# Logits and attention weights kept tap-innermost in SBUF, in a two-layer convolution kernel on one core

## The chip, the cores and the metric

One core of one Trainium2 chip runs the whole batch. The time is device microseconds from the first to the last instruction of one execution; lower is better.

## What is computed

The input x is (32, 56, 56, 96) in float32. Two residual layers follow each other:

```
x = x + L0(group_norm(x))      # outlook attention, 12 heads of 8 channels, 3x3 taps, stride 2
x = x + L1(group_norm(x))      # depthwise 3x3 with the signs of the weights

L0: v = x @ W_v;  the 3x3 patch of v around each of 28x28 windows
    a = mean of each 2x2 pixels of x @ W_a + b_a   -> per window and head a 9x9 matrix
    a = softmax(a * scale) over its last axis (9 taps)
    out[q] = sum_k a[q, k] * v[k];  the 9 outputs are added back to the image at their places
    y = folded @ W_o + b_o
```

What matters here is the matrix a: per image 784 windows, and for each 12 heads x 9 rows q (108 partitions) with 9 taps k.

## The kernel before

One program per engine, each a loop over the images; a body of the loop has 64 slots (g), one per pair of terms of the attention sum. An image goes through a pipeline of stages in three neighbouring bodies: input and logits (`s1`), attention (`s2`), the depthwise layer and output (`cv`). The image is cut into two halves h: half 0 has 15 rows of windows (420 windows), half 1 has 14 (392).

In each slot TensorE broadcasts two weight planes from `stack` to 96 channels (`broadcast`, L733), VectorE multiplies them with the values (`product`, L600, into one of four buffers `prod`), GpSimd adds the two products of 45 of the 64 slots (`pre_add`, L363), and three slots later TensorE multiplies with W_o and accumulates (`add_up`, L753). VectorE waits for the broadcast and for a free buffer; TensorE waits for the pre-added product.

Everything else is put between the slots by hand: the table `AT` names for every kind of piece the slots after which it is issued (numbers from 64 on lie in the next body). Each engine executes in order, and every piece counts up a semaphore that later pieces on other engines wait for. The softmax of one half of one image is this chain:

- logits: TensorE, one matmul per tap (L698) into one of two PSUM banks `side`; ScalarE drains each with the bias into `att[h]` (L433), 9 per half, at slots 19 to 23 for half 0 and 39 to 53 for half 1
- maximum: VectorE, 4 reductions per half over the 9 taps (L623), each a quarter of the windows; slots 24 to 27 and 56 to 58
- less the maximum: GpSimd, 9 pieces (L345); exponential: ScalarE, 3 pieces (L464)
- sum: VectorE, 4 reductions (L627), slots 36 to 39 and 70 to 73; inverse: VectorE, 2 reciprocals (L631); scaled by ScalarE (L467)
- times the inverse: GpSimd, 9 pieces (L351), slots 44 to 49 and 75 to 84
- split into two float16 parts: the first part by ScalarE (L475, 3 pieces), the second part = att - first part by GpSimd (L356, 9 pieces), slots 48 to 54 and 81 to 88
- SyncE copies both parts into `stack` (L283, L289, 12 transfers per half), from which the next attention stage broadcasts.

`att[h]` is laid out as 9 tap planes of 420 or 392 windows, so a piece of GpSimd or ScalarE is one plane or three. A reduction over the taps therefore steps from plane to plane: 1680 bytes in half 0, 1568 in half 1.

On VectorE there are also 24 taps of the depthwise layer per image (L647, both inputs in SBUF), and the additions of a finished class into X1 (L611). ScalarE loads the next image from PSUM (L440), drains the values (L426), starts X1 and ACC and runs the norms; GpSimd adds pixels for the pooling (L332, L338) before the multiplications of half 1.

## Time and profile before

| | |
|---|---|
| median of 3 runs | 5119.74 us (5117.42 to 5121.8) |
| span of the profiled execution, its own time | 5120.9 us |
| TensorE busy | 4119.3 us (80%) |
| VectorE busy | 4730.3 us (92%) |
| ScalarE busy | 2005.6 us (39%) |
| GpSimd busy | 4037.2 us (79%) |
| mean granted TensorE clock | 0.850 of full |

PE is TensorE (PEld its weight loads), DVE VectorE, ACT ScalarE, POOL GpSimd, SP SyncE. Busy time is the union of an engine's instruction times; an instruction that is held up after it has started counts as busy. One image takes about 156 us, so 32 images and some filling make the span.

### The profile page before, as it was taken

The numbers are of one execution on the slowest core, as the hardware profiler recorded it, in microseconds if no ns is written. First come the engines' busy times: TensorE is split into PE (matmuls) and PEld (weight loads), VectorE is DVE, ScalarE is ACT, GpSimd is POOL, SyncE is SP. The second block draws the span as 40 slices with busy tenths as digits, with TensorE's granted clock in tenths as the row PEclk, the third lists the DMA queues.
The fourth block names the chain that finished last, engine by engine and source line by source line (L and its number), as shares of the span: only waits on it lengthen the run. The fifth ranks groups of instructions, "written<-read, shape, count | busy, mean of one in ns | idle before, by whom it ended". The sixth has DMA issues, their size and how long they took to land.

```text
span 5120.9 us, 55367 instructions
## 1 busy us (share of the span) xinstructions
PE 4119.3 (80%) x13632; PEld 2114.1 (41%) x13632; DVE 4730.3 (92%) x3723; ACT 2005.6 (39%) x2753; POOL 4037.2 (79%) x3628
## 2 busy tenths in 40 slices
PE   4877887878887888878788887888878888878885
PEld 2434444434444344444344443444434444434442
DVE  5799999999999999999999999999999999999997
ACT  4424444334443344432444433444324444334431
POOL 5787877877877888778878788787787787887883
PEclk7988888888888788888888888888888888888887
DMA  1110111101111111111011111111110111111111
GB/s 39 38 38 24 47 44 37 47 21 40 47 33 47 36 25 47 42 39 47 21 40 47 33 47 30 31 47 38 43 47 15 46 47 33 47 24 37 47 29 28
DMA packets 126083, 194.36 MB, mean 38 GB/s; under 512 B 14248, under 2 KB 115464, under 8 KB 122472
## 3 DMA queue, kind: packets, MB, share of 16 engines
q1 hardware_dynamic: 97384, 155.50, 13.0%
q10 hardware_dynamic: 28672, 38.55, 2.5%
q8 instruction: 11, 0.18, 0.0%
q14 instruction: 16, 0.13, 0.0%
HBM read 39.22 MB, written 38.54 MB: 15 GB/s over the span
## 4 chain that ended last, share of the span: by engine, by line
POOL 45%; issue 25%; PE 18%; ACT 5%; DVE 5%; DMA 1%; SPq 0%; DVEq 0%; POOLq 0%; ACTq 0%; PEldq 0%; PEld 0%
POOL prod L363 15%; POOL part L356 10%; POOL att L351 10%; PE acc L753 10%; POOL att L345 6%; PE bc L733 4%; DVE prod L600 2%; ACT X L440 2%; POOL pc L332 2%; PE side L698 2%; ACT X L523 2%; PE side L692 1%; DVE ACC L647 1%; PE side L710 1%; DVE top L631 1%
## 5 line engine op out<-in xcount | busy, mean ns | idle before, releaser
L753 PE MATMUL acc<-prod,wo 96*96 96x392 f32 x5312 | 2478.5, 573 | 161.8 <-POOL prod L363 155.7
L600 DVE TENSOR_TENSOR prod<-bc,VAL 96x784 f32<-96x784 f32 x2048 | 1928.2, 959 | 307.5 <-PE bc L733 289.4
L363 POOL TENSOR_TENSOR prod<-prod 96x392 f32<-96x392 f32 x1440 | 1685.5, 1178 | 501.3 <-DVE prod L600 491.7
L733 PE MATMUL bc<-stack,sel 96*96 96x392 f16 x4608 | 1303.2, 378 | 633.5 <-DVE prod L600 611.5
L647 DVE SCALAR_TENSOR_TENSOR ACC<-XP,sg,ACC 96x1064 f32<-96x1064 f32 (+1 forms) x768 | 1736.2, 2281 | 14.9 <-ACT ACC L534 13.8
L753 PEld LDWEIGHTS acc<-prod,wo 96*96 96x96 f32 x5312 | 982.1, 188 | 675.1 <-issue 271.6
L733 PEld LDWEIGHTS bc<-stack,sel 96*96 96x96 f16 x4608 | 576.2, 137 | 1571.4 <-DVE prod L600 972.2
L351 POOL TENSOR_TENSOR att<-att,top 108x420 f32<-108x420 f32 (+1 forms) x576 | 750.3, 1321 | 38.3 <-ACT top L467 38.3
L345 POOL TENSOR_TENSOR att<-att,top 108x420 f32<-108x420 f32 (+1 forms) x576 | 645.1, 1138 | 144.2 <-DVE top L623 144.2
L356 POOL TENSOR_TENSOR part<-att,part 108x420 f16<-108x420 f32 (+1 forms) x576 | 737.3, 1298 | 0.0
L433 ACT ACTIVATE att<-side,ba 108x420 f32<-108x420 f32 (+1 forms) x576 | 340.5, 597 | 671.6 <-PE side L698 659.0
L698 PE MATMUL side<-pooled,wa 96*108 96x392 f32 (+1 forms) x1152 | 528.0, 573 | 46.3 <-ACT att L433 23.2
L627 DVE TENSOR_REDUCE top<-att 108x105 f32<-108x945 f32 (+1 forms) x256 | 456.9, 1796 | 14.5 <-ACT att L464 14.5
L623 DVE TENSOR_REDUCE top<-att 108x105 f32<-108x945 f32 (+1 forms) x256 | 449.3, 1786 | 15.4 <-ACTq L247 13.2
L426 ACT ACTIVATE VAL<-side 96x392 f32<-96x392 f32 (+1 forms) x256 | 124.7, 512 | 857.5 <-DVE prod L600 713.5
L475 ACT ACTIVATE part<-att 108x1260 f16<-108x1260 f32 (+1 forms) x192 | 234.5, 1221 | 470.4 <-POOL att L351 470.2
L698 PEld LDWEIGHTS side<-pooled,wa 96*108 96x108 f32 x1152 | 221.6, 197 | 305.4 <-issue 224.0
L446 ACT ACTIVATE tok_out<-side 112x384 f32<-112x384 f32 x224 | 110.2, 492 | 605.7 <-PE side L710 304.6
L464 ACT ACTIVATE att<-att 108x1260 f32<-108x1260 f32 (+1 forms) x192 | 232.4, 1210 | 140.5 <-POOL att L345 140.5
L692 PE MATMUL side<-XN,wv 96*96 96x392 f32 (+1 forms) x512 | 244.1, 573 | 7.8 <-ACT tok_out L446 3.8
L370 POOL TENSOR_TENSOR gve<-eps,gvar 96x1 f32<-96x1 f32 x64 | 13.2, 206 | 281.8 <-ACT spill L451 268.8
L440 ACT ACTIVATE X<-side 96x448 f32<-96x448 f32 x224 | 204.2, 1000 | 29.4 <-PE side L704 28.2
(55 smaller groups left out, 2183.7 us busy)
## 6 DMA issues: line engine op xcount, KB each, us to landing
stack<-part SPq DMA_DIRECT2D x192, 275.3 KB
stack<-part SPq DMA_DIRECT2D x192, 256.9 KB
tok_in<-in_x SPq DMA_DIRECT2D x32, 1176.0 KB, 9.7
out<-tok_out ACTq DMA_DIRECT2D x224, 168.0 KB, 4.2
stack<-part SPq DMA_DIRECT2D x192, 30.5 KB
stack<-part SPq DMA_DIRECT2D x192, 28.5 KB
X<-in_L_conv_W_a SPq DMA_DIRECT2D x1, 364.5 KB
ACC<-select SPq DMA_DIRECT2D x1, 144.0 KB
```

The source lines that it names most:

```text
L345: nc.gpsimd.tensor_tensor(att[h][:, k, :], att[h][:, k, :], top[h][:, :], ALU.subtract).then_inc(fine_step, 1)
L351: nc.gpsimd.tensor_tensor(att[h][:, k, :], att[h][:, k, :], top[h][:, :], ALU.mult).then_inc(fine_step, 1)
L356: nc.gpsimd.tensor_tensor(low, a4(h)[:, k], high, ALU.subtract).then_inc(fine_step, 1)
L363: nc.gpsimd.tensor_tensor(p[:, 0, :], p[:, 0, :], p[:, 1, :], ALU.add).then_inc(pre_added, 1)
L433: ins = nc.scalar.activation(att[h][:, k, :], bank[0:QN, 0:cols], ACT.Identity, bias=ba[:, k:k + 1])
L600: nc.vector.tensor_tensor(prod[:, g % PRODUCTS, :, :].rearrange("c a (i j) -> c a i j", j=WIN), b, v, ALU.mult).then_inc(prod_ready, 1)
L623: ins = nc.vector.tensor_reduce(top[h][:, c], by_window[:, c, :], AX.X, ALU.max)
L627: ins = nc.vector.tensor_reduce(top[h][:, c], by_window[:, c, :], AX.X, ALU.add)
L647: nc.vector.scalar_tensor_tensor(a, XP[:, r0 + ty:r1 + ty, tx:tx + SIDE], sg[:, t:t + 1], a, ALU.mult, ALU.add).then_inc(tapped, 1)
L698: last = nc.tensor.matmul(bank[0:QN, 0:ROWS[h] * WIN], wa[:, k, :, :], pooled[:, 0:ROWS[h], :], start=True, stop=True)
L733: last = nc.tensor.matmul(bc[g % 2][0:CH, a, 0:UNIT], sel[:, which, :], stack[h][:, qi, ki * TAPS + kj, si:si + HALF, sj:sj + WIN], start= ...
L753: last = nc.tensor.matmul(acc[c % 2][0:CH, 0:UNIT], wo[:, :], prod[:, g % PRODUCTS, a, :], start=first, stop=s == LAST[c] and (g in PRE or ...
```

## The change

`att[h]` is laid out with the windows outside and the 9 taps inside, so the taps of a window are neighbours (4 bytes apart) and the windows 36 bytes apart. The pieces on GpSimd and ScalarE that were planes become groups of window rows (`ROW_CUTS`: two rows or one, so 504 or 252 elements; three of them together make 1260 or 1008). The maximum and the inverse are repeated over the taps by an access pattern with step 0. The logits of a tap are written with a step of 36 bytes, and both float16 parts, whose own layout stays (tap planes), are made from `att` read with that step. The drain of the first logits waits for the last second part of the image before, where each drain waited for that of its own tap. The slots in `AT` are as they were.

```diff
+ROW_CUTS = ((0, 2, 4, 5, 7, 9, 10, 12, 14, 15), (0, 2, 3, 5, 6, 8, 9, 11, 12, 14))
...
-        att = [sb(f"att{h}", [QN, KK, ROWS[h] * WIN]) for h in range(2)]
+        att = [sb(f"att{h}", [QN, ROWS[h] * WIN, KK]) for h in range(2)]
...
         def a4(h):
-            return att[h][:, :, :].rearrange("r k (i j) -> r k i j", j=WIN)
+            return att[h][:, :, :].rearrange("r (i j) k -> r k i j", j=WIN)
+
+        def rows_of(h, n, many=1):
+            return slice(ROW_CUTS[h][n * many], ROW_CUTS[h][(n + 1) * many])
+
+        def columns_of(h, n, many=1):
+            r = rows_of(h, n, many)
+            return slice(r.start * WIN, r.stop * WIN)
+
+        def over_taps(t):
+            return bass.AP(t.tensor, t.offset, [*t.ap, [0, KK]])
...
-                    nc.gpsimd.tensor_tensor(att[h][:, k, :], att[h][:, k, :], top[h][:, :],
+                    c = columns_of(h, k)
+                    nc.gpsimd.tensor_tensor(att[h][:, c, :], att[h][:, c, :], over_taps(top[h][:, c]),
                                             ALU.subtract).then_inc(fine_step, 1)
...
-                    nc.gpsimd.tensor_tensor(att[h][:, k, :], att[h][:, k, :], top[h][:, :],
+                    c = columns_of(h, k)
+                    nc.gpsimd.tensor_tensor(att[h][:, c, :], att[h][:, c, :], over_taps(top[h][:, c]),
                                             ALU.mult).then_inc(fine_step, 1)
...
-                    low, high = (parts[p][:, k, 0:ROWS[h], 0:WIN] for p in (1, 0))
-                    nc.gpsimd.tensor_tensor(low, a4(h)[:, k], high,
+                    r = rows_of(h, k)
+                    low, high = (parts[p][:, :, r, 0:WIN] for p in (1, 0))
+                    nc.gpsimd.tensor_tensor(low, a4(h)[:, :, r], high,
                                             ALU.subtract).then_inc(fine_step, 1)
...
-                    until(act, fine_step, done(FINE, i - 1, LOW, h, k))
-                    ins = nc.scalar.activation(att[h][:, k, :], bank[0:QN, 0:cols],
+                    if k == 0:
+                        until(act, fine_step, done(FINE, i - 1, LOW, h, KK - 1))
+                    ins = nc.scalar.activation(att[h][:, :, k], bank[0:QN, 0:cols],
                                                ACT.Identity, bias=ba[:, k:k + 1])
...
-                    a = att[h][:, 3 * n:3 * n + 3, :]
+                    a = att[h][:, columns_of(h, n, 3), :]
...
-                    ins = nc.scalar.activation(parts[0][:, 3 * n:3 * n + 3, 0:ROWS[h], 0:WIN], a4(h)[:, 3 * n:3 * n + 3],
+                    r = rows_of(h, n, 3)
+                    ins = nc.scalar.activation(parts[0][:, :, r, 0:WIN], a4(h)[:, :, r],
                                                ACT.Identity)
...
-                by_window = att[h][:, :, :].rearrange("r k n -> r n k")
...
-                    ins = nc.vector.tensor_reduce(top[h][:, c], by_window[:, c, :], AX.X, ALU.max)
+                    ins = nc.vector.tensor_reduce(top[h][:, c], att[h][:, c, :], AX.X, ALU.max)
...
-                    ins = nc.vector.tensor_reduce(top[h][:, c], by_window[:, c, :], AX.X, ALU.add)
+                    ins = nc.vector.tensor_reduce(top[h][:, c], att[h][:, c, :], AX.X, ALU.add)
```

## Rows read from the trace of the kernel before

**Rows 1.** The page: busy time and share of the span, by engine.
```profile
PE 4119.3 (80%) x13632; PEld 2114.1 (41%) x13632; DVE 4730.3 (92%) x3723; ACT 2005.6 (39%) x2753; POOL 4037.2 (79%) x3628
```

**Rows 2.** The page: the chain that ended last, share of the span by engine.
```profile
POOL 45%; issue 25%; PE 18%; ACT 5%; DVE 5%; DMA 1%; SPq 0%; DVEq 0%; POOLq 0%; ACTq 0%; PEldq 0%; PEld 0%
```

**Rows 3.** The taps by their line: count, then min/median/max in ns.
```profile
L647 DVE SCALAR_TENSOR_TENSOR ACC<-XP,sg,ACC x768: 1247/2004/6940, 257.4 to 5107.4; 96x1064 f32<-96x1064 f32 x128, 96x1008 f32<-96x1008 f32 x64
```

**Rows 4.** The timeline of VectorE, three taps in a row: start us, us.
```profile
2537.52 10.85 DVE L647 SCALAR_TENSOR_TENSOR ACC<-XP,sg,ACC 96x1064 f32<-96x1064 f32 x3
```

**Rows 5.** One image in stretches A to H: us, busy us by engine.
```profile
core 0: us, PE busy (x) PEld busy (x) DVE busy (x) ACT busy (x) POOL busy (x), PEclk, DMA share, GB/s
2408.90:2417.40 8.50, 7.00 (x36) 4.78 (x36) 8.50 (x8) 2.10 (x5) 5.52 (x6) 0.91 0.57 151
2417.40:2436.20 18.80, 18.80 (x69) 10.54 (x68) 12.24 (x15) 10.23 (x12) 16.77 (x17) 0.86 0.43 109
2436.20:2450.00 13.80, 11.79 (x55) 7.01 (x54) 13.80 (x13) 13.20 (x22) 5.58 (x10) 0.88 0.00 0
2450.00:2482.70 32.70, 28.43 (x89) 13.96 (x89) 30.98 (x23) 19.39 (x27) 29.11 (x27) 0.90 0.04 8
2482.70:2494.00 11.30, 7.98 (x23) 3.50 (x21) 11.30 (x10) 0.00 (x0) 7.94 (x8) 0.85 0.50 111
2494.00:2515.30 21.30, 15.22 (x46) 6.99 (x46) 20.99 (x18) 7.15 (x8) 21.21 (x15) 0.92 0.05 11
2515.30:2533.00 17.70, 14.87 (x49) 7.54 (x49) 17.70 (x17) 3.51 (x6) 10.51 (x11) 0.90 0.00 0
2533.00:2565.20 32.20, 23.18 (x70) 11.14 (x69) 32.10 (x23) 6.98 (x9) 30.12 (x24) 0.79 0.14 34
```

**Rows 6.** VectorE's groups by form: count, then busy us and mean ns of one.
```profile
L600 DVE TENSOR_TENSOR prod<-bc,VAL 96x784 f32<-96x784 f32 x2048 | 1928.2, 959 | 307.5 <-PE bc L733 289.4 <-issue 10.7 <-ACT VAL L426 0.3
...
L623 DVE TENSOR_REDUCE top<-att 108x105 f32<-108x945 f32 x128 | 229.3, 1832 | 2.2 <-ACT att L433 2.1
...
L623 DVE TENSOR_REDUCE top<-att 108x98 f32<-108x882 f32 x128 | 220.0, 1741 | 13.2 <-ACTq L247 13.2
L611 DVE TENSOR_TENSOR X<-acc,X 96x392 f32<-96x392 f32 x256 | 141.1, 551 | 11.2 <-PE acc L753 11.0
```

**Rows 7.** GpSimd's lines, one by one: min/median/max in ns.
```profile
L356 POOL TENSOR_TENSOR part<-att,part x576: 889/951/2069, 79.1 to 4995.3; 108x420 f16<-108x420 f32 x96, 108x392 f16<-108x392 f32 x96
...
L332 POOL TENSOR_TENSOR pc<-X x64: 1483/1584/2462, 24.8 to 4868.6; 96x840 f32<-96x840 f32 x32, 96x784 f32<-96x784 f32 x32
...
L338 POOL TENSOR_TENSOR pooled<-pc x64: 1011/1044/1090, 26.5 to 4871.2; 96x420 f32<-96x420 f32 x32, 96x392 f32<-96x392 f32 x32
...
L363 POOL TENSOR_TENSOR prod<-prod x1440: 998/1016/2104, 101.3 to 5061.3; 96x392 f32<-96x392 f32 x180
```

**Rows 8.** ScalarE's groups by form: a strided and a packed drain.
```profile
L440 ACT ACTIVATE X<-side 96x448 f32<-96x448 f32 x224 | 204.2, 1000 | 29.4 <-PE side L704 28.2 <-ACT X L523 0.2
...
L426 ACT ACTIVATE VAL<-side 96x448 f32<-96x448 f32 x96 | 48.9, 543 | 718.3 <-DVE prod L600 713.5 <-PE side L692 2.8 <-ACT tok_out L446 2.0
```

**Rows 9.** The second parts (L356) in E and H: busy us, count.
```profile
2482.70:2494.00 11.30, 3.52 (x4) 0.85 0.50 111
2533.00:2565.20 32.20, 12.00 (x8) 0.79 0.14 34
```

**Rows 10.** Timelines of ScalarE and VectorE, logits and first maxima of half 0.
```profile
2468.91 1.32 ACT L433 ACTIVATE att<-side,ba 108x420 f32<-108x420 f32 x2 [2.44 <-PE side L698]
2470.12 1.18 ACT L475 ACTIVATE part<-att 108x1176 f16<-108x1176 f32 x1
...
2478.84 1.29 ACT L433 ACTIVATE att<-side,ba 108x420 f32<-108x420 f32 x2
...
2482.74 3.60 DVE L623 TENSOR_REDUCE top<-att 108x105 f32<-108x945 f32 x2
```

**Rows 11.** Timelines of SyncE and VectorE: last copy, first product of half 1.
```profile
2493.03 0.78 SPq L289 DMA_DIRECT2D stack<-part  x1
...
2504.34 0.96 DVE L600 TENSOR_TENSOR prod<-bc,VAL 96x784 f32<-96x784 f32 x1
```

## The prediction, made before the changed kernel was run

> **What bounds the kernel now.** I read the busy shares first. VectorE is busy 92% of the span, TensorE 80%, GpSimd 79% [rows 1]: three engines are near their limit, so the share alone names no bound. The chain of waits says more: 45% of it runs through GpSimd and only 5% through VectorE [rows 2]. The reason shows where both meet. A tap (L647) takes 1.25 us at best and 2.0 in the middle [rows 3], yet three of them in a row lasted 10.85 us [rows 4], with GpSimd busy all the while. A tap reads two operands in SBUF, and so does a GpSimd piece; here they run one after the other. Much of VectorE's 92% is therefore a wait for GpSimd, and where taps stand, the time is the sum of both.
>
> The period of one image is some 156 us. I cut one into eight stretches [rows 5]: A maxima of half 1, B values, C sums and inverses of half 1, D multiplications and second parts of half 1 with taps and the logits of half 0, E maxima of half 0, F subtractions with taps, G sums and inverses of half 0, H multiplications and second parts of half 0 with taps. VectorE is full in A, C, E and G, where the sixteen reductions lie (four in each). TensorE is full in B. GpSimd is nearly full in F and H, and busy 29.1 of 32.7 us in D.
>
> My sum is made per image and times 32, against the profiled span of 5120.9 us; the median of the runs, 5119.74, stands 1.2 below it, which I leave out.
>
> **The reductions (gain).** Before, the nine taps of a window lie 1680 or 1568 bytes apart; after, they are neighbours. A maximum takes 1832 ns for 945 elements and 1741 for 882, 1787 in the mean, and a sum as much within 12 ns [rows 6]. VectorE's operations with short steps take 551 ns for 392 elements and 959 for 784 [rows 6]: 1.04 ns an element and 143 ns beside. By that, 945 elements take 1127 and 882 take 1061, mean 1094. I take 0.69 us saved of each, 2.8 in each stretch. The other bound is nothing saved, if the time belongs to the reduction and not to its step.
>
> What of it reaches the end is what the next engine leaves. A: TensorE is busy 7.0 of 8.5 us, so 1.5. C: ScalarE is busy 13.2 of 13.8 us (loading the next image, starting X1), and GpSimd's pooling and the multiplications queued behind it wait for that, so 0.6. E: TensorE 8.0 and GpSimd 7.9 of 11.3, so 2.8. G: TensorE 14.9 of 17.7, so 2.8. Together 7.7 us an image.
>
> **The second part on GpSimd (loss).** L356 now reads the logits 36 bytes apart, 18 times an image, each 951 ns in the middle [rows 7]. No row shows GpSimd at such a step. L332 reads 8 bytes apart and shows no penalty (784 elements in 1483 ns, against 998 for 392 in L363 [rows 7]). Bounds: nothing, or even -0.26 us (L332's 1.9 ns an element against 2.55, times 406); above, ScalarE's ratio. Its strided write (L440, 112 bytes) takes 1000 ns where a packed one takes 543 [rows 8]: 1.84 times, so 0.80 us more. I take the surcharge per element of VectorE's reductions, the nearest strided read: (1832-1127)/945 = 0.75 ns, times 406 elements = x = 0.31 us. Of the 18 pieces, 4 start in E and 8 in H [rows 9], one in A and so 5 in D. In D and H GpSimd has no cover, 13x = 4.0. In E the 7.9 us of GpSimd grow by 4x past the 8.5 left after the gain: 4x-0.56 = 0.7. In A it is hidden (5.5 us of 8.5). Sum 4.7 us. SyncE's copies into the stack (L283, L289) follow the last piece; the last is issued at 2493.0 us and TensorE's next half feeds a product at 2504.3 [rows 11], so a shift of 1 to 3 us is covered; without that cover it would cost those 1 to 3 us.
>
> **Subtraction and multiplication.** The same elements in nine pieces of 504 or 252 instead of 420 or 392; one operand is repeated nine times. I take nothing. Lower bound: two operands on the same few bytes, as in L332, -0.25 us each, -9 an image. Upper: short runs. L338 reads 14 runs and takes 1011 ns at least, L363 one run and takes 998 [rows 7], about 1 ns a run, so 0.05 us each and 1.8 an image. They lie on the path, without cover.
>
> **ScalarE (small loss).** L433 now writes 36 bytes apart and L475 reads so. By L440 against the packed drain, (1000-543)/448 = 1.02 ns an element [rows 8]: a logits drain goes from 0.6 to 1.04 us, a first part from 1.19 to 2.4. In D, from 2468.9 to 2480.1 us [rows 10], nine drains and two first parts take 7.9 us; they would take 14.2, 3.0 beyond the 11.2 there. The maxima start 2.6 us after the last drain [rows 10], so they come 0.4 late; TensorE, which has two banks for these tiles, waits some 0.6 for drains, and behind it in order stand broadcasts that VectorE needs. I take 1.0 us an image; bounds 0 and 3.0. In H, ScalarE is busy 7 of 32 us and covers it.
>
> **Edits at nothing.** The drain of logits 0 now waits for the last second part of the image before, not for its own. That part is over at the start of A for half 0 and at 2487.6 us for half 1, while those logits come in D and in G: 30 us of cover. Exponentials and first parts wait for three row pieces as they did for three tap pieces. The pieces of 1260 and 1008 elements in the place of 1176 sum to the same.
>
> **Sum.** -7.7 + 4.7 + 1.0 = -2.0 us an image, times 32 = -64: 5057 us. By this formula the change is neither gain nor loss at x = 0.43 (17x - 0.56 = 6.7).
>
> **Rivals.**
> 1. *The second part pays in proportion.* Place: L356 in D, E, H, on GpSimd, with taps behind it. If a strided read costs GpSimd the ratio that it costs VectorE, 1787/1094 = 1.63, x is 0.60: 17x-0.56 = 9.6, net +2.9 an image, +93: 5214. It decides from x = 0.43 on. With ScalarE's 0.80 it is +202: 5323. For it: GpSimd's chain share; against: L332 pays nothing at 8 bytes. Chance 0.17. Between the surcharge and the ratio, a second part half as long again (x = 0.48) gives 17x-0.56 = 7.6, +0.9 an image, +29: 5150, slower too; chance 0.13.
> The Trainium skill, GPSIMD Engine Reference, Performance pitfalls, states that a step over 8 bytes makes a read loop about 50% dearer. By that x is that of the half-as-long-again case, and the change loses; no row here shows such a step.
> 2. *The reductions do not get faster,* their time belonging to the operation. Then 13x + 1.0 = 5.0 an image, +160: 5281. For it: the 63 elements between the two forms cost 91 ns, 1.4 each and not 1.8, so something beside the step is in it; against: 0.7 us more than other operations of the size. Chance 0.10.
> 3. *Reads at 36 bytes are free* on GpSimd and ScalarE. Then -7.7 + 0.5 = -7.2 an image, -230: 4891. For it: L332. Chance 0.16.
> 4. *The gain is all taken elsewhere* (TensorE in A and G, the taps): within 0.2%. Chance 0.04.
>
> **How the numbers follow.** The forecast has 0.40, with 4990 to 5110 as its own range (x from 0.1 to 0.43, ScalarE from 0 to 2). 0.2% is about what a measurement can tell from no change. Faster: 0.38 of the forecast's 0.40 and 0.16, so 0.54. Slower: 0.29 of rival 1's 0.30 (both cases) and 0.10, so 0.39. Same: the rest, 0.07. The range goes from 4870, just below rival 3, to 5290, just above rival 2; it leaves out ScalarE's ratio on GpSimd and a cheap repeated operand, some 2 in 10 with what I have not seen.
>
> **What would show it.** Right: L623 and L627 near 1.1 us, L356 near 1.26, L345 and L351 with the busy time they had, L433 near 1.0, L475 near 2.4; VectorE's share falls under 88%, its wait for TensorE's broadcasts grows, GpSimd's wait for products shrinks, GpSimd's share of the chain rises. Wrong: L356 at 1.4 or more (rival 1), reductions at 1.8 (rival 2), L356 unchanged (rival 3), or L345 and L351 moved by more than 0.1 us in the mean, which would outweigh all the rest.

## The result, and the profile after

The changed kernel takes 5239.57 us (median of 4 runs, 5221.27 to 5259.17) against 5120.71 for the kernel before on the same chip: 1.023 times as long, with a 95% interval from 1.021 to 1.026. It is slower by 119 us, where I had forecast 64 us faster. The profiled execution took 5259.17 us, with a span of 5257.4, which is 136.5 more than the span before.

The page: busy time by engine, and the chain's shares [rows 1, 2].

```profile
span 5257.4 us, 54863 instructions
PE 4145.8 (79%) x13632; PEld 2138.0 (41%) x13632; DVE 4544.1 (86%) x3723; ACT 2400.8 (46%) x2753; POOL 3950.3 (75%) x3628
...
POOL 30%; PE 28%; issue 19%; DVE 8%; ACT 6%; DMA 5%; ACTq 1%; SPq 1%; DVEq 0%; POOLq 0%; PEld 0%; PEldq 0%
```

VectorE is busy 186 us less than before and GpSimd 87 us less. Only ScalarE has more work, and it is the idlest of the four. So the two engines that I had called the limit got lighter, and the kernel got slower.

The groups by form: count, then busy us and mean ns of one, then the idle time before them.

```profile
L662 DVE SCALAR_TENSOR_TENSOR ACC<-XP,sg,ACC 96x1064 f32<-96x1064 f32 x512 | 1401.4, 2738 | 14.8 <-ACT ACC L550 14.0 <-DVE ACC L662 0.8
...
L370 POOL TENSOR_TENSOR part<-att,part 108x504 f16<-108x504 f32 x352 | 575.1, 1638 | 0.5 <-ACT part L491 0.5
L364 POOL TENSOR_TENSOR att<-att,top 108x504 f32<-108x504 f32 x352 | 449.0, 1283 | 36.5 <-ACT top L482 36.5
L357 POOL TENSOR_TENSOR att<-att,top 108x504 f32<-108x504 f32 x352 | 448.9, 1283 | 59.5 <-DVE top L638 59.4
L491 ACT ACTIVATE part<-att 108x1260 f16<-108x1260 f32 x160 | 396.9, 2481 | 312.5 <-POOL att L364 312.5
L448 ACT ACTIVATE att<-side,ba 108x420 f32<-108x420 f32 x288 | 267.7, 1005 | 125.0 <-PE side L713 125.0
L370 POOL TENSOR_TENSOR part<-att,part 108x252 f16<-108x252 f32 x224 | 251.6, 1123 | 0.0
L638 DVE TENSOR_REDUCE top<-att 108x105 f32<-108x945 f32 x128 | 138.6, 1122 | 7.3 <-ACT att L448 7.1
L638 DVE TENSOR_REDUCE top<-att 108x98 f32<-108x882 f32 x128 | 132.5, 1056 | 15.8 <-ACTq L258 15.8
```

L638 answers to L623 before, L448 to L433, L491 to L475, L370 to L356, L357 and L364 to L345 and L351, L662 (the taps) to L647. The reductions take 1122 and 1056 ns, where I had 1127 and 1061. Among the groups that were not touched, the taps of this form grew most: 1222 us before, 1401 after (the other form, 96x1008, fell from 529 to 494).

The waits: us in total, times, the longest.

```profile
POOL prod L377 <- DVE prod L616: 828.2, 523, 7.5
...
DVE prod L616 <- PE bc L748: 550.3, 560, 4.8
```

Before, GpSimd waited 491.7 us for products and VectorE 289.4 us for broadcasts. Both now wait more: no engine is busy throughout, they wait for one another.

**Where in an image.** Each image makes 64 products, one per slot, and their starts show how long every slot took. This table is worked out from them, as a mean over 28 images. The last column is the duration of the five last taps, at slots 50, 50, 52, 53 and 53. The kernels marked * are experiments of the next section.

```
us per image  period  0-13  14-23 24-35 36-47 48-54 55-63 | last five taps
before        156.95  26.40 29.71 32.60 21.90 26.81 19.53 | 2.44 1.95 1.31 2.10 1.95
after         161.88  26.45 29.34 28.13 21.70 33.93 22.34 | 5.07 2.37 1.31 6.92 1.78
*e1           151.05  25.83 30.29 29.98 20.35 26.82 17.78 | 2.44 1.95 1.31 2.10 1.95
*e11          166.04  26.14 30.84 30.93 20.89 35.25 21.98 | 5.68 2.16 1.31 6.68 2.16
*e2           150.23  26.25 28.73 28.16 21.63 27.94 17.52 | 4.04 1.65 1.31 2.08 2.63
*e14          157.27  27.16 33.39 29.58 20.69 29.45 17.00 | 5.48 2.07 1.31 1.31 2.07
*e10          147.89  26.07 28.19 28.23 30.84 15.95 18.61 | taps at 43 to 47, all 1.22 to 1.81
```

Up to slot 47 the changed kernel gains 5.0 us an image. From slot 48 on it loses 9.9. The 4.9 us between them, over 28 images, make up the 137 us that the spans differ by. Two taps carry most of the 9.9: the first at slot 50 went from 2.44 to 5.07 us, and the first at slot 53 from 2.10 to 6.92, for 1.3 us of work each.

The timeline of the changed kernel there shows how. VectorE first, then GpSimd over the same time (start us, us, and in brackets the idle time before it and what ended it).

```profile
2601.91 7.37 DVE L662 SCALAR_TENSOR_TENSOR ACC<-XP,sg,ACC 96x1064 f32<-96x1064 f32 x2
2609.21 1.84 DVE L616 TENSOR_TENSOR prod<-bc,VAL 96x784 f32<-96x784 f32 x2
2610.98 1.31 DVE L662 SCALAR_TENSOR_TENSOR ACC<-XP,sg,ACC 96x1064 f32<-96x1064 f32 x1
2612.21 0.96 DVE L616 TENSOR_TENSOR prod<-bc,VAL 96x784 f32<-96x784 f32 x1
2613.09 8.62 DVE L662 SCALAR_TENSOR_TENSOR ACC<-XP,sg,ACC 96x1064 f32<-96x1064 f32 x2
```
```profile
2602.16 0.61 POOL L364 TENSOR_TENSOR att<-att,top 108x252 f32<-108x252 f32 x1
2602.74 1.40 POOL L370 TENSOR_TENSOR part<-att,part 108x504 f16<-108x504 f32 x1
2604.10 1.02 POOL L377 TENSOR_TENSOR prod<-prod 96x392 f32<-96x392 f32 x1
2605.07 3.15 POOL L370 TENSOR_TENSOR part<-att,part 108x252 f16<-108x252 f32 x2
2611.13 2.03 POOL L377 TENSOR_TENSOR prod<-prod 96x392 f32<-96x392 f32 x1 [2.91 <-DVE prod L616]
2613.12 2.12 POOL L370 TENSOR_TENSOR part<-att,part 108x504 f16<-108x504 f32 x2
2615.21 1.01 POOL L377 TENSOR_TENSOR prod<-prod 96x392 f32<-96x392 f32 x1
2616.18 4.47 POOL L370 TENSOR_TENSOR part<-att,part 108x504 f16<-108x504 f32 x3
2623.56 1.02 POOL L377 TENSOR_TENSOR prod<-prod 96x392 f32<-96x392 f32 x1 [2.91 <-DVE prod L616]
```

The pair of taps from 2601.91 lasts until GpSimd has nothing left that is ready. The first tap takes 5.07 us of it: four pieces begin and end before it gets in (L364, L370, L377 and the first of two L370, together 3.8 us). The fifth then waits for it, and GpSimd stands still for 2.91 us afterwards, because the product it wants next is queued on VectorE behind those taps. The same comes again at 2613.09, where five of six pieces pass (two L370, L377 and two of three L370). GpSimd has run ahead in its second parts while VectorE made no product, and then both engines lose the time in turn. The tail is TensorE's: its transposes of the output (L725) wait for the last tap, with the next broadcasts queued behind them.

```profile
2621.77 0.90 PE L725 MATMUL side<-idn,ACC 96*112 96x96 f32 x4 [5.08 <-DVE ACC L662]
```

Over the run that is 167.8 us of waiting before L725's matmuls and 150.4 before their weights, against 53.8 and 27.1 before; slot 60 alone is 3.8 us longer.

In slots 55 to 63 the granted clock is lower too. Here is one image's stretch before, then one of the changed kernel: time in us, each engine's busy us and instructions, then the granted TensorE clock as a share of full.

```profile
2563.00:2582.90 19.90, 17.48 (x68) 10.18 (x68) 15.89 (x17) 4.23 (x9) 15.22 (x16) 0.83 0.64 164
...
2458.90:2481.10 22.20, 19.10 (x68) 11.40 (x68) 13.27 (x17) 4.18 (x9) 10.93 (x12) 0.73 0.53 145
```

The same 68 matmuls keep TensorE busy 1.6 us longer. Over every second of the 28 images the clock there is 0.83 against 0.75 (means between the two levels, 1.2 and 2.4 GHz) and TensorE is busy 17.7 against 18.9 us. In the seven slots just before, TensorE had been idle longer, 13.9 against 8.5 us in these two images. So up to 1.3 of the 2.8 us that these slots lose goes with a lower clock; no run holds the clock fixed to separate it.

In the kernel before, the same two pairs of taps and the GpSimd pieces beside the first pair were these.

```profile
2550.06 4.32 DVE L647 SCALAR_TENSOR_TENSOR ACC<-XP,sg,ACC 96x1064 f32<-96x1064 f32 x2
...
2558.20 3.97 DVE L647 SCALAR_TENSOR_TENSOR ACC<-XP,sg,ACC 96x1064 f32<-96x1064 f32 x2
```
```profile
2550.32 1.06 POOL L351 TENSOR_TENSOR att<-att,top 108x420 f32<-108x420 f32 x1
2551.35 1.98 POOL L356 TENSOR_TENSOR part<-att,part 108x420 f16<-108x420 f32 x1
2553.28 1.98 POOL L363 TENSOR_TENSOR prod<-prod 96x392 f32<-96x392 f32 x1
```

There a piece and a tap took turns. A second part of 0.94 us reads as 1.98, because it waited for a tap in its turn. Each of these taps let one piece past, not four or five.

But the kernel before has a tap that is held as long as any after the change: the first of the three at slot 48. It takes 6.93 us in the mean of the images, and 5.94 in the changed kernel. It is the beginning of the 10.85 us of [rows 4]. This is GpSimd over that time, and all but the last of these pieces end before the tap gets in, five of six.

```profile
2538.25 1.00 POOL L363 TENSOR_TENSOR prod<-prod 96x392 f32<-96x392 f32 x1
2539.22 2.10 POOL L351 TENSOR_TENSOR att<-att,top 108x420 f32<-108x420 f32 x2
2541.28 1.02 POOL L363 TENSOR_TENSOR prod<-prod 96x392 f32<-96x392 f32 x1
2542.27 3.11 POOL L351 TENSOR_TENSOR att<-att,top 108x420 f32<-108x420 f32 x2
```

All 24 taps together last 55.9 us an image before and 60.6 after, for some 31 us of work. The change did not bring held taps into the kernel: it added two, at slots 50 and 53, and eased others (the first tap of the image, at slot 14, went from 5.03 to 2.89 us).

The Trainium skill, SBUF — State Buffer, SBUF: two separate sides, calls the pair of ports that the two engines share an exclusive lock: whichever starts first holds it for its whole instruction and the other blocks. That fits one piece passing a tap. It says nothing of a tap that stays blocked while four or five pieces begin one after the other, which is what the rows above show. Nor does the order of the starts decide there: the tap's record begins at 2601.91, before that of L364 at 2602.16, and yet L364 takes its shortest time, 0.61 us, and the tap 5.07.

### The profile page after: what moved, and what is told of

It is laid out like the page before. It is cut to its first block, busy times and chain, and to the rows that moved or that the text cites. A ratio compares the mean times of both kernels' runs of the same rounds, so it can differ in the third digit from the quotient of the medians.

```text
span 5257.4 us, 54863 instructions
## 1 busy us (share of the span) xinstructions
PE 4145.8 (79%) x13632; PEld 2138.0 (41%) x13632; DVE 4544.1 (86%) x3723; ACT 2400.8 (46%) x2753; POOL 3950.3 (75%) x3628
## 4 chain that ended last, share of the span: by engine, by line
POOL 30%; PE 28%; issue 19%; DVE 8%; ACT 6%; DMA 5%; ACTq 1%; SPq 1%; DVEq 0%; POOLq 0%; PEld 0%; PEldq 0%
PE acc L768 14%; POOL prod L377 10%; PE bc L748 7%; POOL part L370 6%; POOL att L357 6%; DVE ACC L662 5%; POOL att L364 5%; DMA out<-tok_out 5%; PE side L713 4%; ACT X L455 2%; DVE prod L616 2%; POOL pc L343 2%; ACT X L539 2%; PE side L725 1%; PE side L707 1%
## 5 line engine op out<-in xcount | busy, mean ns | idle before, releaser
L377 POOL TENSOR_TENSOR prod<-prod 96x392 f32<-96x392 f32 x1440 | 1629.2, 1136 | 834.4 <-DVE prod L616 828.2
L662 DVE SCALAR_TENSOR_TENSOR ACC<-XP,sg,ACC 96x1064 f32<-96x1064 f32 (+1 forms) x768 | 1880.2, 2468 | 15.0 <-ACT ACC L550 14.0
L370 POOL TENSOR_TENSOR part<-att,part 108x252 f16<-108x252 f32 (+1 forms) x576 | 817.2, 1438 | 0.5 <-ACT part L491 0.5
L448 ACT ACTIVATE att<-side,ba 108x420 f32<-108x420 f32 (+1 forms) x576 | 531.4, 980 | 621.7 <-PE side L713 621.7
L357 POOL TENSOR_TENSOR att<-att,top 108x252 f32<-108x252 f32 (+1 forms) x576 | 636.7, 1124 | 59.5 <-DVE top L638 59.4
L364 POOL TENSOR_TENSOR att<-att,top 108x252 f32<-108x252 f32 (+1 forms) x576 | 635.3, 1121 | 36.5 <-ACT top L482 36.5
L713 PE MATMUL side<-pooled,wa 96*108 96x392 f32 (+1 forms) x1152 | 567.1, 610 | 96.0 <-ACT att L448 72.3
L491 ACT ACTIVATE part<-att 108x1260 f16<-108x1260 f32 (+1 forms) x192 | 461.2, 2403 | 312.9 <-POOL att L364 312.5
L725 PE MATMUL side<-idn,ACC 96*112 96x96 f32 x896 | 159.1, 325 | 268.7 <-DVE ACC L662 167.8
L642 DVE TENSOR_REDUCE top<-att 108x105 f32<-108x945 f32 (+1 forms) x256 | 276.6, 1091 | 54.1 <-ACT att L479 54.1
L638 DVE TENSOR_REDUCE top<-att 108x105 f32<-108x945 f32 (+1 forms) x256 | 271.1, 1089 | 23.0 <-ACTq L258 15.8
L725 PEld LDWEIGHTS side<-idn,ACC 96*112 96x112 f32 x896 | 133.2, 202 | 360.0 <-DVE ACC L662 150.4
```

What stands on the lines that cost most here:

```text
L357: nc.gpsimd.tensor_tensor(att[h][:, c, :], att[h][:, c, :], over_taps(top[h][:, c]), ALU.subtract).then_inc(fine_step, 1)
L364: nc.gpsimd.tensor_tensor(att[h][:, c, :], att[h][:, c, :], over_taps(top[h][:, c]), ALU.mult).then_inc(fine_step, 1)
L370: nc.gpsimd.tensor_tensor(low, a4(h)[:, :, r], high, ALU.subtract).then_inc(fine_step, 1)
L377: nc.gpsimd.tensor_tensor(p[:, 0, :], p[:, 0, :], p[:, 1, :], ALU.add).then_inc(pre_added, 1)
L448: ins = nc.scalar.activation(att[h][:, :, k], bank[0:QN, 0:cols], ACT.Identity, bias=ba[:, k:k + 1])
L491: ins = nc.scalar.activation(parts[0][:, :, r, 0:WIN], a4(h)[:, :, r], ACT.Identity)
```

## The experiments

All are timed beside the kernel before on the same chip (its medians there: 5119.5 to 5124.7 us). Ratios are to it, with 95% intervals.

**Which part of the change costs: e1 to e4.** e1 is the kernel before with reductions that read neighbours. e2, e3 and e4 are the changed kernel with its second part, with ScalarE's accesses, and with both read or written packed. All four work on as many elements as before, but on others than the softmax wants.

```diff
e1 (before)
-                by_window = att[h][:, :, :].rearrange("r k n -> r n k")
+                by_window = att[h][:, :, :].rearrange("r k n -> r (k n)").rearrange("r (n k) -> r n k", k=KK)
e2, e4 (after)
-                    nc.gpsimd.tensor_tensor(low, a4(h)[:, :, r], high,
+                    nc.gpsimd.tensor_tensor(low, packed(h, k), high,
e3, e4 (after)
-                    ins = nc.scalar.activation(att[h][:, :, k], bank[0:QN, 0:cols],
+                    ins = nc.scalar.activation(flat[:, k * cols:(k + 1) * cols], bank[0:QN, 0:cols],
...
-                    ins = nc.scalar.activation(parts[0][:, :, r, 0:WIN], a4(h)[:, :, r],
+                    ins = nc.scalar.activation(parts[0][:, :, r, 0:WIN], packed(h, n, 3),
```

> The kernel before, with one edit: the 512 reductions read nine neighbouring elements instead of one element of each of nine planes, so they reduce other numbers than the softmax wants. Nothing else moves. Theory A (the strided accesses of the change are paid in full): the reductions fall to 1.09 us and the time falls by what my sum gave for them, 7.7 us an image, to about 4875 us. Theory B (two taps that find GpSimd in an unbroken row of pieces decide, and how long they wait depends on when they come): the time is not tied to the reductions; H keeps its length only if the taps of slots 48 to 53 arrive in the same order with the pieces, else it grows by some microseconds: anywhere from 4875 to 5100 us, with the difference in slots 48 to 60.

> The changed kernel, with the logits read packed in the second part on GpSimd (other elements than its place wants). Theory A: the second part costs 0.2 us less each (1.39 to about 1.2 us for 504 elements), 18 times 32 of them: 115 us less, about 5125 us. Theory B: the pieces are shorter, but what counts is whether the taps of slots 50 and 53 still wait 5.1 and 6.9 us; if they do, the time stays within 60 us of 5240; if they fall back to 2.4 and 2.1, it falls by 200 us or more, to 5040 or below.

> The changed kernel, with ScalarE writing the logits packed and reading packed for the first part (other places and elements than wanted). ScalarE's 400 us of extra busy time go. Theory A': TensorE waits in slots 19 to 25 for the slow drains (slots 19, 20, 23 and 25 are longer by 4.4 us an image than before): 90 to 140 us less, 5100 to 5150 us. Theory B: 0 to 60 us less, since the taps of slots 50 and 53 stay as they are.

> The changed kernel with both edits: no strided access is left, only the cut by rows, the repeated operand and the fast reductions differ from before. Theory A: the gain of the reductions and of the cheaper subtraction and multiplication stands alone: 4880 us or less. Theory B: still above 4950 us, with taps of slots 48 to 53 that wait for GpSimd's row of pieces longer than before.

| | median us | ratio |
|---|---|---|
| e1 | 4944.49 | 0.967 (0.964 to 0.969) |
| e2 | 4915.78 | 0.961 (0.959 to 0.963) |
| e3 | 5242.66 | 1.022 (1.018 to 1.026) |
| e4 | 4990.61 | 0.972 (0.968 to 0.976) |

The short reductions alone are worth 179 us (5123.47 - 4944.49), or 5.6 us an image. ScalarE's strided accesses cost nothing (e3 against after, 3 us). The strided second part is more than the whole loss: packed, it brings 324 us (after against e2) and, with ScalarE packed, 252 (e3 against e4). Its own work changes far less. At their shortest its pieces take 1.36 and 0.77 us strided, 1.10 and 0.64 packed, so 0.26 x 352 + 0.13 x 224 = 121 us in all. Even e2 still has a held tap (4.04 us at slot 50); the one at slot 53 is gone (2.08), and slots 55 to 63, at a mean granted clock of 0.95 against 0.75 after, are 4.8 us shorter. That e4, with less work on ScalarE than e2, takes 75 us more shows the same sensitivity: there the first tap at slot 53 is held again, for 3.88 us. Theory B's statements came out for e2, e3 and e4. For e1 its range, 4875 to 5100, was too wide to test anything.

**Is it the stride, or what the stride does to the taps: e11.** It is e1 with GpSimd's second part reading 36 bytes apart. The drains wait as in the changed kernel; the profile shows no idle time behind that wait. It reads other logits of the same planes; pieces, counts and order are those of e1.

```diff
e11 (e1)
-                    nc.gpsimd.tensor_tensor(low, a4(h)[:, k], high,
+                    t, of = att[h][:, 3 * (k // 3), :], (7 if h else 3)
+                    nine = bass.AP(t.tensor, t.offset, [t.ap[0], [0, of], [KK * WIN, ROWS[h] // of], [KK, WIN]])
...
+                    nc.gpsimd.tensor_tensor(low, nine, high,
...
-                    until(act, fine_step, done(FINE, i - 1, LOW, h, k))
+                    if k == 0:
+                        until(act, fine_step, done(FINE, i - 1, LOW, h, KK - 1))
```

> The kernel before with packed reductions (4944 us in an experiment above) and one thing more: the second part on GpSimd reads 420 or 392 logits 36 bytes apart (others than its place wants). Pieces stay tap planes. Theory A (paid as work): the second part costs 0.2 to 0.3 us more, times 576 = 115 to 170 us: 5060 to 5115 us. Theory B (what the longer pieces do to the taps behind them): not tied to that; the taps of slots 48 to 53 wait longer by more than the sum of the surcharges: 5120 to 5250 us.

It took 5378.22 us, 1.050 (1.048 to 1.052): 434 us more than e1, and above the ranges of both theories; B was right in kind and too low by 130 us. A piece of 420 takes 1.15 us at its shortest, against 0.94 in e1: 0.21 us x 576 = some 120 us. By the products' starts, 8.4 of the 15.0 us an image between the two stand in slots 48 to 54 and 4.2 in slots 55 to 63. In the latter the granted clock was 0.73 against 0.93 in e1, and TensorE was busy 19.5 against 15.6 us: most of these 4.2 us go with the clock. e1's taps at slots 50 and 53 (VectorE's timeline), and then the same two pairs in e11:

```profile
2300.71 4.32 DVE L647 SCALAR_TENSOR_TENSOR ACC<-XP,sg,ACC 96x1064 f32<-96x1064 f32 x2
...
2308.84 3.97 DVE L647 SCALAR_TENSOR_TENSOR ACC<-XP,sg,ACC 96x1064 f32<-96x1064 f32 x2
```
```profile
2500.12 7.76 DVE L651 SCALAR_TENSOR_TENSOR ACC<-XP,sg,ACC 96x1064 f32<-96x1064 f32 x2
...
2511.69 8.76 DVE L651 SCALAR_TENSOR_TENSOR ACC<-XP,sg,ACC 96x1064 f32<-96x1064 f32 x2
```

And the group of the second part in e1, then in e11.

```profile
L356 POOL TENSOR_TENSOR part<-att,part 108x420 f16<-108x420 f32 x288 | 421.6, 1482 | 0.0
```
```profile
L359 POOL TENSOR_TENSOR part<-att,part 108x420 f16<-108x420 f32 x288 | 421.5, 1482 | 0.0
```

This pair is the trap of the case. The pieces with 0.2 us more work in each show the same busy time to 0.1 us. In e1 part of it was waiting for a tap; in e11 the pieces wait less and the taps more. So this group looks untouched, while VectorE's taps grow. It holds for half 0's pieces alone: those of half 1 (392 elements) went from 342.1 to 400.8 us, which is their own 0.21 us more.

**Is it the stride, or length alone: e14.** It is e1 with a second part that subtracts another operand, the scale in float32, so that it stays packed but takes 1.06 us in the place of 0.94. That operand is another in type and place too, so length is not quite the only difference. The maxima also wait for the last second part of the image before, which is long over by then.

```diff
e14 (e1)
+                    high = top[h][:, :].rearrange("r (i j) -> r i j", j=WIN)
                     nc.gpsimd.tensor_tensor(low, a4(h)[:, k], high,
...
-                        until(dve, fine_step, done(FINE, home - 1, MUL, h, KK - 1))
+                        until(dve, fine_step, done(FINE, home - 1, LOW, h, KK - 1))
```

> The kernel before with packed reductions (4944 us) and a second part that subtracts the float32 scale in the place of the float16 first part: read packed, but longer, by GpSimd's other float32 pieces 1.06 us for 420 elements in the place of 0.94 (the strided read made it 1.15 and the time 5378 us). If the length is what holds the taps, the taps of slots 50 and 53 wait longer by microseconds here too, and the time rises by more than the 65 us of the work: 5060 to 5378 us. If the strided read itself does it: 4944 plus at most 65, 4940 to 5010 us, with the waits of those taps as before (2.4 and 2.1 us).

5131.70 us, 1.001 (1.000 to 1.003), in the range given for length: 187 us more than e1 for 0.12 us x 576 = some 70 us of work. The first pair of taps is held, the second is not:

```profile
2387.83 7.47 DVE L648 SCALAR_TENSOR_TENSOR ACC<-XP,sg,ACC 96x1064 f32<-96x1064 f32 x2
...
2399.11 3.31 DVE L648 SCALAR_TENSOR_TENSOR ACC<-XP,sg,ACC 96x1064 f32<-96x1064 f32 x2
```

So a packed piece that is longer does it too, and in steps: at 1.06 us the pair at slot 50 is held, at 1.15 (e11) both are. The table shows 2.6 us of e14's loss in slots 48 to 54; another 3.1 stands in slots 14 to 23. There lie the second parts of half 1, and there too taps are held: the one at slot 19 takes 3.14 us in the mean and the first at slot 20 4.76, against 1.57 and 1.25 in e1.

**Does it hang on one tap and one piece: e12.** The row groups of half 0 come in another order, so that short pieces stand where long ones stood.

```diff
-ROW_CUTS = ((0, 2, 4, 5, 7, 9, 10, 12, 14, 15), (0, 2, 3, 5, 6, 8, 9, 11, 12, 14))
+ROW_CUTS = ((0, 1, 3, 5, 6, 8, 10, 11, 13, 15), (0, 2, 3, 5, 6, 8, 9, 11, 12, 14))
```

> The changed kernel with the nine row pieces of half 0 in the order 1, 2, 2 rows instead of 2, 2, 1 in each group of three: the same elements, the same number of pieces, the same groups of three. Theory A: the work is the same, so 5240 us within 30. Theory B: the two held taps meet GpSimd's row of pieces at another point; their waits of 3.8 and 5.6 us change by a microsecond or more, and the time moves with them by 50 us or more, either way.

5239.14 us, 1.023 (1.020 to 1.025), the time of the changed kernel. The pair at slot 50 took 1.50 and 5.72 us in the place of 5.07 and 2.37, the first at slot 53 took 6.92 us as in the changed kernel. The time lies in theory A's range, and theory B's 50 us did not come; that A is wrong follows from e2 and e11, not from here. Between these two orders of the pieces another tap of the pair is held, at about the same price. Looking for a luckier order of pieces was a miss.

**Can the pieces get out of the way: e5, e7, e8.** The second parts of half 0 come later (e5), that and the nine last taps spread over slots 40 to 53 (e7), and both in the kernel before (e8).

```diff
e5, e7 (after), e8 (before)
-    LOW: ((48, 49, 51, 51, 52, 52, 53, 54, 54), (81, 81, 84, 84, 85, 87, 88, 88, 88)),
+    LOW: ((48, 49, 52, 52, 53, 55, 56, 57, 58), (81, 81, 84, 84, 85, 87, 88, 88, 88)),
e6, e7 (after), e8 (before)
-    "taps": (14, 17, 18, 18, 19, 20, 20, 21, 25, 29, 30, 31, 32, 34, 35, 45, 48, 48, 48, 50, 50, 52, 53, 53),
+    "taps": (14, 17, 18, 18, 19, 20, 20, 21, 25, 29, 30, 31, 32, 34, 35, 40, 42, 45, 46, 48, 49, 50, 52, 53),
```

> The changed kernel with seven of the nine second parts of half 0 issued later on GpSimd: slots 52, 52, 53, 55, 56, 57, 58 in the place of 51, 51, 52, 52, 53, 54, 54. The work is the same; GpSimd now meets a product that it must wait for earlier, so its unbroken row of pieces in front of the taps of slots 50 and 53 is shorter. Theory B (the held taps decide): those two taps wait 2 to 4 us less each, and the time falls by 4 to 7 us an image, to between 5010 and 5110 us. Theory A (the second part's strided read is paid as work): the same work in another place, 5240 us within 30.

> The changed kernel with both moves. Theory B: at least as fast as the better of the two, 4900 to 5050 us, and so under the kernel before. Theory A: 5240 us within 30.

> The kernel before (tap planes, reductions of 1.79 us) with both moves: does the new order help by itself? Theory B with VectorE full in stretch G: the two taps moved there lengthen G by what they take from H, so 5080 to 5150 us, about as before; the moves are worth something only where the reductions are short. If it falls under 5050 us, the order was simply a bad one for both kernels and the gain of the two experiments above is not owed to the change.

e5: 5222.06 us, 1.019 (1.015 to 1.023). The first tap at slot 50 fell to 3.35 us and the first at 53 to 4.25; slots 48 to 54 came down to 29.8 us. But slot 63 rose by 5 us and slots 0 and 1 by 2.4: the copies into the stack follow the last second part, and the next stage's broadcasts wait for them. The loss mostly moved. e7: 5105.47 us, 0.998 (0.996 to 0.999); e8: 5262.69 us, 1.029 (1.027 to 1.030). All three forecasts of theory B failed. e5 even lies in theory A's range, though its taps did get shorter; e7 lies between the two ranges; e8 is 113 us above its own. In e8 slots 36 to 54 take as long as before, and the loss stands in slots 55 to 63 (2.9 us an image) and 0 to 13 (1.4), as in e5: later pieces seem to cost the kernel before as well, though no run has them alone there.

**Can the taps get out of the way: e6, e9, e10.** The same nine taps are moved ahead of the second parts, by steps: spread (e6, diff above), seven before slot 48 (e9), all before slot 48 (e10). Nothing else is changed.

```diff
e9:  "taps": (..., 34, 35, 38, 40, 42, 44, 45, 46, 47, 50, 52)
e10: "taps": (..., 34, 35, 36, 38, 40, 42, 43, 44, 45, 46, 47)
```

> The changed kernel with the last nine taps on VectorE at slots 40, 42, 45, 46, 48, 49, 50, 52, 53 in the place of 45, 48, 48, 48, 50, 50, 52, 53, 53. The work is the same; two taps move to where GpSimd had nothing to do and VectorE has room since the reductions are short, and no slot holds two. Theory B: 5 to 9 us less an image, 4950 to 5080 us. Theory A: 5240 us within 30, since no second part is cheaper.

> The changed kernel with the last nine taps at slots 38, 40, 42, 44, 45, 46, 47, 50, 52: seven ahead of the stretch where GpSimd has a row of ready pieces, two in it. If a tap costs its own 1.3 us where GpSimd is idle and 4 to 5 us in that row (measured for slots 48, 50, 53 with the taps spread), three fewer in the row save up to 10 us there and cost 4 us before it: 4 to 6 us an image less than with the taps spread (5045 us), so 4850 to 4930 us. If the taps' place doesn't matter beyond their sum: 5045 us within 30.

> The changed kernel with all nine last taps at slots 36, 38, 40, 42, 43, 44, 45, 46, 47, none in the row of second parts. VectorE then bounds slots 36 to 47 (up to 4 us an image more there than with seven early), GpSimd alone bounds slots 48 to 54. 4820 to 4950 us; if the place of the taps doesn't matter: 5045 us.

e6: 5044.57 us, 0.982 (0.975 to 0.988). e9: 4872.77, 0.953 (0.950 to 0.955). e10: 4845.29, 0.946 (0.944 to 0.947), the fastest of all, 5.4% below the kernel before and 7.5% below the changed one. All three came out as theory B or the estimate from e6 had it. e6 still has taps at slots 50 and 53 that last 3.9 and 5.4 us; among e10's nine the longest lasts 1.8 us in the mean.

The page, two groups and one wait of e10, against those of after above:

```profile
PE 3966.2 (82%) x13632; PEld 2039.3 (42%) x13632; DVE 4016.1 (83%) x3723; ACT 2407.0 (50%) x2753; POOL 3989.2 (82%) x3628
...
L377 POOL TENSOR_TENSOR prod<-prod 96x392 f32<-96x392 f32 x1440 | 1716.7, 1199 | 432.0 <-DVE prod L616 418.8 <-issue 0.3
L662 DVE SCALAR_TENSOR_TENSOR ACC<-XP,sg,ACC 96x1064 f32<-96x1064 f32 x512 | 967.4, 1890 | 15.2 <-ACT ACC L550 14.0 <-DVE ACC L662 0.5
```
```profile
POOL prod L377 <- DVE prod L616: 418.8, 325, 7.6
```

VectorE's busy time falls by 528 us for the same instructions: the taps of this form alone give back 434 (1401.4 to 967.4). GpSimd waits half as long for products, and 82% of its span is busy, more than before the change. On the timeline a tap now stands alone between other operations of VectorE, and over the same time GpSimd waits 4.08 us for a product (last line):

```profile
2235.68 1.31 DVE L662 SCALAR_TENSOR_TENSOR ACC<-XP,sg,ACC 96x1064 f32<-96x1064 f32 x1
2236.91 0.96 DVE L616 TENSOR_TENSOR prod<-bc,VAL 96x784 f32<-96x784 f32 x1
2237.79 1.12 DVE L642 TENSOR_REDUCE top<-att 108x105 f32<-108x945 f32 x1
2238.84 0.96 DVE L616 TENSOR_TENSOR prod<-bc,VAL 96x784 f32<-96x784 f32 x1
2239.72 1.25 DVE L662 SCALAR_TENSOR_TENSOR ACC<-XP,sg,ACC 96x1008 f32<-96x1008 f32 x1
...
2239.87 3.07 POOL L377 TENSOR_TENSOR prod<-prod 96x392 f32<-96x392 f32 x2 [4.08 <-DVE prod L616]
```

**Is that the change's gain or the taps' own: e13.** The kernel before, with e10's taps.

> The kernel before with the last nine taps at slots 36, 38, 40, 42, 43, 44, 45, 46, 47, as in the fastest kernel so far (4845 us with the changed layout). If the two belong together (VectorE is full in slots 36 to 39 with reductions of 1.79 us, and the taps there delay the products that GpSimd and TensorE wait for): 4990 to 5130 us, at least 145 us above 4845. If the taps' place alone did it: about 4845 us plus the reductions' 180 us at most, and clearly under the kernel before; if it comes under 4900 us, the change of layout has no part in the gain.

5159.44 us, 1.007 (1.005 to 1.010), 29 us above the range for "the two belong together" and so on its side: the taps' place alone did not do it. Its slots 48 to 54 fall from 26.8 to 17.8 us, but slots 36 to 47 grow from 21.9 to 31.9, where eight taps more now stand. The forecast's reason, that the long sums leave those slots no room, is not what the times show: in the changed kernel the same move costs them nearly as much, from 21.7 to 30.8 us. What differs is what the move takes away. In slots 48 to 63 it is 9.0 us an image here and 21.7 there, because there more taps were held. With the taps early the change of layout is worth 314 us (e13 against e10), where it cost 119 with the taps as they were. How much of the 314 the short reductions alone would bring was not run.

## Why the prediction was wrong

**Its sizes were right or too pessimistic.** The reductions saved 0.71 and 0.69 us (0.69 forecast). The logits drain takes 1.005 us (1.04 forecast) and the first part 2.48 (2.4). The second part, where nothing holds it, takes 0.22 us more than before in the mean (eleven pieces of 1.36 and seven of 0.77 us in eighteen make 1.13, against 0.91), where I had x = 0.31. Subtraction and multiplication, at nothing in my sum, became cheaper: 1.045 us for 504 elements and 0.61 for 252, a mean of 0.88 against 1.03 before, towards my lower bound; L364 is busy 642.9 us, L351 was 750.3. "Moved by more than 0.1 us" was one of my signs of being wrong; it came, on the side of the gain, and did not outweigh the rest.

**Put into my formula, these sizes take it further from the measured time.** -7.7 + (17 x 0.22 - 0.56) + 1.0 = -3.5 us an image, and with 36 pieces cheaper by 0.15 us -8.9: some 4835 us. The kernel took 5240. So mis-sized pieces are not the cause; the structure of the sum was wrong.

**The step that failed** is the one that prices the second part: "In D and H GpSimd has no cover, 13x = 4.0". It adds the extra time of each piece once to the path and leaves the taps as they were. I had shown in [rows 4] that taps and GpSimd pieces run one after the other and had written that "the time is the sum of both"; then I took the order in which they get in as fixed. It is not. In the changed kernel the first taps at slots 50 and 53 took 5.07 and 6.92 us in the place of 2.44 and 2.10, and slots 48 to 63 lost 9.9 us an image, where the formula with x = 0.22 has 3.2 us for the second part wherever it stands. The sign was in my own rows: of the 10.85 us of three taps the first alone took most, because five pieces passed it. With e11 the price of x = 0.21 is 434 us, 13.6 us an image, where my formula gives 17 x 0.21 - 0.56 = 3.0. With e14 the price of 0.12 is 5.8 where the formula gives 1.5. The price comes in jumps, by how many pieces of the row pass a tap that would otherwise take turns with them. Some of it is TensorE's, at the lower granted clock of slots 55 to 63.

**The gain was real, but smaller.** I had 7.7 us an image at the end; e1 shows 5.6, the changed kernel has 5.0 by slot 47. ScalarE's 1.0 us was nothing (e3). The edits at nothing showed no wait of their own.

**Rival 1** came out on the right side for a reason that was not its own. It wanted x of 0.48 or more; x was 0.22, below its deciding point of 0.43, and GpSimd did not become the limit: it is 75% busy and its share of the chain fell from 45% to 30%. The rule of the Trainium skill (GPSIMD Engine Reference, Performance pitfalls) of reads half as dear again, which I gave beside it, is not borne out for this operation: the same piece took 0.94 us packed and 1.15 strided, 23% more. Rival 2 is refuted by the reductions. Rival 3, that the strided reads are free, is refuted by sizes, and yet e10 goes below its time. Rival 4, a gain taken up elsewhere to within 0.2%, is refuted by the time.

**The signs I had named** split in the same way. VectorE's share under 88% (86%) and its longer wait for broadcasts came. GpSimd's wait for products was to shrink and grew from 491.7 to 828.2 us; its chain share was to rise and fell. These two speak of the order between the engines, and they were what a forecast about order would have had to get right.

**What is shown and what is open.** Shown: the loss comes with the longer second part (e2, e3), stride or not (e11, e14); it stands in held taps and what waits behind them; taps placed ahead of GpSimd's row take it away and leave a gain (e9, e10), which the same move without the change does not have (e13). Not separated: what the granted clock adds. Its mean over the run was 0.850 before, 0.843 after, 0.864 in e1 and 0.893 in e10, and in slots 55 to 63 it goes with most of the difference between e1 and e11. Open: the rule by which a waiting tap gets in at one boundary between two pieces and not at the next. In the kernel before the first tap at slot 48 got in after five pieces and those at slots 50 and 53 after one, here the latter after four or five, and e12 moved it by one tap. I have only the durations, and tried nothing that measures that rule by itself.

## What to carry to other kernels

Where two engines exclude each other on a shared resource, busy times must not be summed: ask for each operation that needs it whether the other engine then has a row of ready work, and who waits for the one that loses. A piece that grows by 0.1 or 0.2 us in such a row can cost about three times its work, as in e11 and e14. And place the blocked operations anew, away from the other engine's busy stretch, even if they are paid in full where they go: here that turned +2.3% into -5.4%, while the same move without the change gave +0.7%.

## What I had not expected of the hardware

- An operation of VectorE with two operands in SBUF took up to 6.9 us for 1.3 us of work, with five GpSimd pieces beginning and ending meanwhile, before the change and after it.
- GpSimd's subtraction and multiplication got cheaper when one operand is repeated nine times: 504 elements in 1.045 us, where 420 had taken 1.06.
- A read 36 bytes apart costs each engine its own surcharge: GpSimd 0.51 ns an element (1.15 against 0.94 us for 420); ScalarE 0.97 (2481 against 1257 ns for 1260), and 0.94 for a write (1005 against 610 ns for 420); VectorE's reductions, from 1680 bytes down to 4, 0.75 (1832 against 1122 ns for 945).
- A group's busy time can stay the same, 421.6 and 421.5 us, while its own work grows by a fifth, if it waits less for the other engine.
